# A selective scan in sixteen chunks: the rows of B and C transposed a chunk earlier, C's columns copied later, and D times x moved from a GpSimd addition into the first two products

## What is computed

```python
dA = exp(dt * A)              # A: (heads, 8)
dB = dt * Bt
def step(h, (dA_t, dB_t, x_t, C_t)):
    h = dA_t * h + dB_t * x_t          # h: (batch, head, 128, 8)
    y_t = einsum('bhds,bhs->bhd', h, C_t)
y = scan(step) + D * x        # D: one number per head
y = y[inverse permutation] * silu(gate) + res
```

## Time and profile before

| | us |
|---|---|
| median of 3 runs (1003.84 to 1005.7) | 1004.92 |
| the profiled execution | 1010.08 |
| its span | 1008.3 |
| of it front, scan, last stage | 255, 230, 523 |
| PE busy in the span | 916.3 |
| POOL busy in the span | 487.7 |

### The profile page before, as it was taken

How to read it: one execution, slowest core, us unless ns; L and a number is a source line. 1 busy time by engine, 2 the same in 40 slices (tenths; PEclk the granted TensorE clock), 3 DMA queues, 4 the chain that set the end, 5 groups by cost and what they waited for, 6 DMA issues and landing times.

```text
span 1008.3 us, 15638 instructions
## 1 busy us (share of the span) xinstructions
PE 916.3 (91%) x4658; PEld 714.5 (71%) x4658; DVE 747.3 (74%) x2003; ACT 534.5 (53%) x1037; POOL 487.7 (48%) x549
## 2 busy tenths in 40 slices
PE   3999899999776787777799999999999999999997
PEld 3887788887454555445678777787777777787776
DVE  5677778564776778666778787788778787788875
ACT  2767677776987998776433332333333332333330
POOL 2145577887788788886544413344034431340000
PEclk8889899999788989778899999999999999999999
DMA  5227765547447444632531401413104131040001
GB/s 171 84 85 215 193 157 171 145 79 234 134 118 171 131 130 124 183 106 86 188 127 43 167 23 39 146 42 144 43 21 166 39 120 70 21 166 21 21 1 42
DMA packets 63690, 110.07 MB, mean 109 GB/s; under 512 B 18539, under 2 KB 44437, under 8 KB 60565
## 3 DMA queue, kind: packets, MB, share of 16 engines
q1 hardware_dynamic: 54388, 90.23, 28.6%
q0 software_dynamic: 7168, 18.03, 6.4%
q10 hardware_dynamic: 2080, 1.19, 0.5%
HBM read 61.51 MB, written 47.92 MB: 109 GB/s over the span
## 4 chain that ended last, share of the span: by engine, by line
PE 66%; DMA 10%; POOL 8%; DVE 6%; issue 4%; SPq 2%; ACT 2%; ACTq 0%; DVEq 0%; POOLq 0%
PE bank L1432 36%; PE bank L1166 8%; PE bank L1341 5%; PE bank L1368 5%; POOL sm L732 4%; DMA bc_scratch<-r 4%; DMA bl<-bc_scratch 3%; PE bank L1396 2%; SPq L460 2%; PE bank L1176 2%; PE bank L1194 2%; PE bank L1380 1%; DMA score_scratch<-score 1%; DVE kbd L1844 1%; DMA xin<-rows_scratch,turn 1%
## 5 line engine op out<-in xcount | busy, mean ns | idle before, releaser
L801 POOL TENSOR_TENSOR ssm<-ssm,rg 128x512 f32<-128x512 f32 x30 | 35.2, 1195 | 255.0 <-DVE ssm L1902 255.0
L1432 PE MATMUL bank<-wexph,xhl 128*128 128x512 f32 x512 | 144.1, 403 | 0.0
L1432 PE MATMUL bank<-wexph,cr 128*128 128x512 f32 x512 | 143.2, 401 | 0.0
L789 POOL DMA_INDIRECT xtm<-y_scratch,idxu x112 | 109.7, 980 | 61.3 <-issue 30.2
L732 POOL TENSOR_TENSOR sm<-sm,rg 128x512 f32<-128x512 f32 x96 | 122.7, 1278 | 29.9 <-DVE rg L1829 17.8
L1829 DVE TENSOR_TENSOR rg<-rg,bank 128x512 f32<-128x512 f32 x112 | 72.4, 679 | 50.5 <-PE bank L1294 43.6
L1432 PEld LDWEIGHTS bank<-wexph,xhl 128*128 128x128 f32 x512 | 93.3, 188 | 22.4 <-DVE xf L2008 1.7
L1432 PEld LDWEIGHTS bank<-wexph,cr 128*128 128x128 f32 x512 | 93.4, 189 | 21.8 <-DVE ysb L2008 1.7
L975 ACT ACTIVATE rg<-dists,aown 128x512 f32<-128x512 f32 x128 | 81.9, 722 | 0.0
L1432 PE MATMUL bank<-wexpl,xhl 128*128 128x512 f32 x256 | 80.7, 396 | 0.0
L1432 PE MATMUL bank<-wexpl,cr 128*128 128x512 f32 x256 | 80.4, 395 | 0.0
(11 more groups left out here) (309 smaller groups left out, 2092.1 us busy)
## 6 DMA issues: line engine op xcount, KB each, us to landing
xin<-in_x SPq DMA_DIRECT2D x16, 1024.0 KB, 5.4
res_gate_scratch<-rg SPq DMA_DIRECT2D x16, 1024.0 KB, 10.6
rg<-res_gate_scratch SPq DMA_DIRECT2D x8, 2048.0 KB
y_scratch<-ysb SPq DMA_DIRECT2D x16, 512.0 KB, 3.7
out<-stage SPq DMA_DIRECT2D x16, 512.0 KB, 2.7
rows_scratch<-stage SPq DMA_DIRECT2D x8, 580.0 KB, 7.2
bc_scratch<-r SPq DMA_DIRECT2D x16, 288.0 KB, 3.9
rows_scratch<-xr SPq DMA_DIRECT2D x6, 580.0 KB, 9.2
```

Of the source, the lines that this page charges most:

```text
L789: pool.indirect_dma_start(out=xtm[:, t, h * P:(h + 1) * P], out_offset=None, in_=y_d[b // GB].rearrange("q p s c -> (q p s) c"), in_offset ...
L1432: last = pe.matmul(bank[4 + i][:, :], x_[:, k, i * P:(i + 1) * P], w[:, 2 * ep * KC + k:2 * ep * KC + k + KC + 1:KC, :], start=(n + k == 0 ...
```

## The change

1. **Rows earlier.** In PE's queue `rows_of(q+2)` stands at the end of chunk q, ahead of `states(q+1)`; before, `rows_of(q+1)` stood behind the first product of chunk q. `rows_high(q+1)` and `block_decays(q+1)` are now the first of ACT's chunk q. The place of `rows_low(q+1)` in DVE's queue is the same. `dec` gets two columns, one for even and one for odd chunks.
2. **Columns later.** `columns(q)` stands on PE behind product 2 of chunk q, on ACT behind the decays of chunk q; before, both were in chunk q-1. It waits for `rows_low(q+1)`, since both use bank 4.
3. **Decays earlier.** ACT's decays 0 and 1 of chunk q+1 move ahead of `y_rows(q-1)` and `up_to_token(q+2)`.
4. **D in the products.** Partitions 64 to 127 of `cr` for states 0 and 1 hold an identity, those of `bl` hold D on the diagonal (state 0) and what rounding left of it (state 1). `dskip` goes, and POOL sums in six additions, the first from two decayed products.
5. **Setup.** `zero_rows` (DVE) has two memsets and two copies of 64x512 in place of one memset (for `cr1` 128x2048 becomes 128x1024 and 64x1024). `skip_rows` (DVE, 8 instructions of 64x64) comes at the end of batch 5.
6. In `last_chunks` ACT's decays of chunk 15 are spread around `z_high` and `columns`; before, all eight stood behind them.

The diff, cut to its core:

```diff
+        dec = sb("dec", [P, 2])
...
 spread(c):
-                sync.wait_ge(a_free.sem, a_free.at(c.q, 1))
+                sync.wait_ge(rows_split.sem, rows_split.at(c.q, 1))
...
 add_state(c, s) on POOL:
-                if s == 0:
-                    pool.wait_ge(dskip_ready, 2)
+                if s == 1:
+                    pool.wait_ge(bc_used[0].sem, bc_used[0].at(c.q, 1))
                     if c.q:
                         pool.wait_ge(k_ready.sem, k_ready.at(c.q - 1, 0))
                 else:
-                    pool.wait_ge(summed.sem, summed.at(c.q, s))
+                    pool.wait_ge(summed.sem, summed.at(c.q, s - 1))
-                pool.tensor_tensor(total, bc(dskip[:, :], 1, ST) if s == 0 else total, new, ALU.add).then_inc(
+                pool.tensor_tensor(ksum[c.two], ee[:, 0, :] if s == 1 else ksum[c.two], ee[:, s, :], ALU.add).then_inc(
                     summed.sem, 1)
...
 body(q) on ACT:
-                decays(c, 0, 2)
-                if q + 1 < CHUNKS:
-                    rows_high(Chunk(q + 1))
-                    block_decays(Chunk(q + 1))
+                rows_high(Chunk(q + 1))
+                block_decays(Chunk(q + 1))
                 if q:
                     decays(c, 2, S)
-                    states_by_tile(c)
-                    for h in range(HEADS):
-                        y_rows(Chunk(q - 1), h)
                 else:
                     decays(c, 2, 4)
                     stage_rows(NB - 1, 0, 1)
                     decays(c, 4, S)
                     stage_rows(NB - 1, 1, 4)
-                    states_by_tile(c)
-                if q + 2 < CHUNKS:
-                    up_to_token(Chunk(q + 2))
-                if q + 1 < CHUNKS:
-                    columns(Chunk(q + 1))
+                columns(c)
+                states_by_tile(c)
+                decays(Chunk(q + 1), 0, 2)
+                if q:
+                    for h in range(HEADS):
+                        y_rows(Chunk(q - 1), h)
+                up_to_token(Chunk(q + 2))
...
 rows_of(c) on PE:
-                pe.wait_ge(a_free.sem, a_free.at(c.q, 0))
+                if c.q:
+                    pe.wait_ge(rows_split.sem, rows_split.at(c.q, 0))
+                    pe.wait_ge(dec_ready.sem, dec_ready.at(c.q, 0))
+                if c.q > 1:
+                    pe.wait_ge(cols_copied.sem, cols_copied.at(c.q - 1, 0))
...
 columns(c) on PE:
-                pe.wait_ge(a_free.sem, a_free.at(c.q, 1))
+                if c.q + 1 < CHUNKS:
+                    pe.wait_ge(rows_split.sem, rows_split.at(c.q + 1, 1))
+                    pe.wait_ge(dec_ready.sem, dec_ready.at(c.q + 1, 1))
+                pe.wait_ge(w_ready.sem, w_ready.at(c.q, 4))
...
 zero_rows(i, b) on DVE:
-                part = cr[0][:, :, :] if i == 0 else cr[1][:, 0:S // 2, :]
-                dve.memset(part.bitcast(F32), 0.0).then_inc(cr_zero[i], 1)
+                dve.memset(cr[i][:, 2:S if i == 0 else S // 2, :].bitcast(F32), 0.0).then_inc(cr_zero[i], 1)
+                dve.memset(cr[i][0:SUB, 0:2, :].bitcast(F32), 0.0).then_inc(cr_zero[i], 1)
+                for j in range(2):
+                    dve.tensor_copy(cr[i][SUB:P, j, :].rearrange("p (t n) -> p t n", n=SUB),
+                                    bc(ident[SUB:P, SUB:P], 1, ST)).then_inc(cr_zero[i], 1)
...
 last_chunks() on ACT:
                 z_high(0)
+                decays(last, 2, 5)
                 columns(last)
-                decays(last, 0, S)
+                decays(last, 5, S)
```

More of the change, by code:

```diff
@@ L756, in body @@
                 c = Chunk(q)
-                for s in range(S - 1):
+                for s in range(1, S - 1):
                     if q == CHUNKS - 2 and s in (S - 3, S - 2):
@@ L904, in columns @@
             def columns(c):
-                act.wait_ge(a_full.sem, a_full.at(c.q, 2))
-                act.activation(cwt[c.four][:, :], bank[A_BANK][:, 0:P], ACT.Copy).then_inc(a_free.sem, 1)
+                act.wait_ge(cols_out.sem, cols_out.at(c.q, 1))
+                act.activation(cwt[c.four][:, :], bank[A_BANK][:, 0:P], ACT.Copy).then_inc(cols_copied.sem, 1)
             def store_rows(b):
@@ L1054, in gate_exp @@
                 act.activation(soft[par][:, 1], soft[par][:, 0], ACT.Exp).then_inc(soft_exp.sem, 1)
-            columns(Chunk(0))
+            decays(Chunk(0), 0, 2)
             for q in range(CHUNKS - 2):
@@ L1065, in last_chunks @@
                 decays(c, 2, S)
+                columns(c)
                 states_by_tile(c)
+                decays(last, 0, 2)
                 for h in range(HEADS):
@@ L1219, in rows_of @@
                 pe.matmul(bank[A_BANK][:, 2 * P:2 * P + 1], args[:, 0, :, :].rearrange("p t c -> p (t c)"), ends[:, :],
[L1220 removed]
+                          start=True, stop=True).then_inc(rows_out.sem, 1)
             def times_of(c):
@@ L1270, in batch @@
                     sums_of(Chunk(1))
+                    rows_of(Chunk(1))
                     states(Chunk(0))
-                    columns(Chunk(0))
             pe.wait_ge(pool_setup, 8)
@@ L1313, in body @@
                 if q + 1 < CHUNKS:
-                    rows_of(Chunk(q + 1))
                     times_of(Chunk(q + 1))
-                products(c, 1, 4)
+                products(c, 1, 3)
+                columns(c)
+                products(c, 3, 4)
                 if q == CHUNKS - 2:
@@ L1334, in body @@
                 products(c, 6, S)
+                if q + 2 < CHUNKS:
+                    rows_of(Chunk(q + 2))
                 if q + 1 < CHUNKS:
                     states(Chunk(q + 1))
-                    columns(Chunk(q + 1))
             def transpose_tiles(dst, src):
@@ L1556, in constants @@
                 own.did(dve.tensor_tensor(aown[:, :], acol[:, 0, :], acol[:, 1, :], ALU.add))
-                for h in range(HEADS):
-                    rr = slice(SUB * h, SUB * h + SUB)
-                    dve.tensor_scalar(dskip[rr, :], ident[rr, rr], dpar[rr, h:h + 1], None, ALU.mult).then_inc(
-                        dskip_ready, 1)
                 own.did(dve.tensor_reduce(own_rows[:, :], ident[:, :].rearrange("p (t x) -> p t x", x=2 * S), AX.X,
@@ L1751, in batch @@
                     rows_by_rank()
+                if b == 5:
+                    skip_rows()
             def flatten(c):
@@ L1821, in next_states @@
                 else:
-                    dve.scalar_tensor_tensor(then[0:SUB, :], now[SUB:P, :], dec[SUB:P, :], add[SUB:P, :],
+                    dve.scalar_tensor_tensor(then[0:SUB, :], now[SUB:P, :], dec[SUB:P, c.two:c.two + 1], add[SUB:P, :],
                                              ALU.mult, ALU.add).then_inc(h_ready.sem, 1)
```

76 lines of the change are left out of this document (44 added, 32 removed).

## The result

| | before | after |
|---|---|---|
| median of 10 runs, us | 1005.09 (1002.5 to 1005.75) | 998.07 (996.37 to 1001.83) |
| after / before | | 0.9932, 95% interval 0.9914 to 0.9949 |
| profiled execution, us | 1010.08 | 1000.0 |
| its span, us | 1008.3 | 998.2 |

The interval is 5.1 to 8.6 us less. The forecast was 4.3 less, at 1000.6: sign and range held, the size fell short by 2.5. The two profiled executions are 10.1 apart, 3 more than the medians, because that of before lay far above its own median. So I took a second trace of the kernel before, and judge each term by both.

The account below looks back on a forecast made before the run. Bound in the scan: a ring of products, store and loads (12.96 us a chunk), with POOL the bound in chunks 11 and 12. Terms -4.4 - 1.25 + 0.3 + 1.1 = -4.25 gave a median of 1000.6 us, range 996.5 to 1003.6.

Parts of the forecast that it names:

- a ring through several engines: Scan, chunks 2 to 9: first product to store, landing, load issues and loads repeat, 12.96 us a chunk.
- moving a producer ahead: Scan: rows moved earlier bring nothing, since `rows_low` still stands behind `whole_kernel` in DVE's queue; link keeps 3.43 us.
- step at the edge of a stage: Start of the scan: two copies in `zero_rows` make the store of chunk 2 1.1 us late (0 to 2).
- Lead and landing: Scan's stores: landing depends on how long before them POOL's gathers began; lead 2.57, landing 3.6; lead 2.1, landing 4.5.

Follow-up runs that it names:

- the order alone: Changed kernel with `dskip`, the seven additions and the old `zero_rows` put back, leaving only the new order: 1004.87 us, 0.9970 to 1.0022 of the kernel before.
- one exchange more: Changed kernel with `rows_low` of the next chunk ahead of `whole_kernel` in DVE's queue: 986.59 us, in a repeat 988.99.
- that exchange without the order: Kernel before with six additions and its old order, plus `rows_low` ahead of `whole_kernel`: 1006.90 us, 0.9985 to 1.0036 of the kernel before.
- nine traces with the old ring: Traces of kernels with `rows_low` behind `whole_kernel`: the kernel before twice, the changed kernel and six follow-up kernels; chunk 4 took 15.1 to 16.9 us in each.

## What to carry to other kernels

When a path is a ring through several engines, moving a producer ahead is worth nothing until its consumer leaves the queue in which it waits behind something else: nothing that could be told for the order alone, about 10 us with one exchange more, and a loss of about 7 for that exchange without the order. Ask of each step at the edge of a stage what it waits for before its cost is added to the path; a millisecond's kernel that differs by 2.6 us from one trace to the next needs a second trace of before for terms of 1 us.

## What was not expected of the hardware

**Lead and landing.** In nine traces with the old ring, the 288 KB store of chunks 2 to 15 without chunk 5 (117 landings) took, by how long before it the nearest pair of gathers had begun (no run moved the gathers alone, so this is what goes together, not a tested cause):

| gathers begun before the store, us | landings | least, median, most, us |
|---|---|---|
| 2.1 to 2.3 | 14 | 4.28, 4.47, 4.92 |
| 2.3 to 2.8 | 27 | 3.42, 3.86, 4.45 |
| 2.8 to 3.3 | 18 | 3.36, 3.59, 4.97 |
| 3.3 to 4 | 20 | 3.09, 3.22, 5.05 |
| over 4 | 38 | 3.06, 3.09, 3.40 |

**A copy on VectorE waits for the end of GpSimd's addition.** The flatten (`bct`, 128x128, SBUF to SBUF) takes 0.28 to 0.31 where no addition of GpSimd runs. I had read the earlier trace rows as 1.24 beside additions and 0.35 without, but that of 0.35 too ended 0.14 after an addition. The trace after the change has a 0.29 in the middle of five additions:

```profile
406.77 0.29 DVE L1782 COPY bct<-xtm 128x128 f32<-128x128 f32 x1
...
421.59 1.08 DVE L1782 COPY bct<-xr 128x128 f32<-128x128 f32 x1
```

The additions of 405.64 on end at 406.92, 408.28 and so on, and those beside 421.59 at 422.52. The copies end at 407.06 and 422.67, 0.14 and 0.15 after. In the three traces of before and after every flatten that started under an addition ended 0.14 to 0.18 after that addition, or after its own 0.28 where that was later; its length only says when in the addition it began. (The Trainium skill, "GPSIMD Engine Reference", Key points, says that GpSimd shares its SBUF interfaces with VectorE, with contention for VectorE instructions in a 2-port perf mode or with two SBUF inputs. The traces agree for this copy.) The copies of `zero_rows` did not wait: two took 0.76 together under a GpSimd instruction of 2.93 us. Why they differ from the flatten no run shows.
